# A router in four column groups, exponentials and scores moved one place forward, and the first expert's opening taken out of the expert programs (gated cross-attention with a mixture of experts, float32, one core)

## What is computed

```python
x = x + tanh(g_xattn) * xattn(layernorm(x), ctx)          # 16 heads of 32, 128 keys
xf = (layernorm(x) * ln_gamma + ln_beta).reshape(T, 512)  # T = 4096
logits = clip(xf @ router_w.T, -10000, 10000)             # (T, 8)
top_v, top_i = top_k(logits, 2)
top_p = exp(top_v - max) / sum
# every token goes to 2 of 8 experts, at most 1280 tokens each
gu = einsum('ecd,efd->ecf', xb, w12); h = silu(g) * u
yb = einsum('ecf,edf->ecd', h, w3)
out[tokens] += weights * yb
x = x + tanh(g_ffn) * out
```

## Time and profile before

| | |
|---|---|
| median of 3 runs | 2671.38 us (2670.05 to 2671.79) |
| the profiled execution's own time | 2672.94 us |
| its span, first to last instruction | 2671.2 us |
| PE busy | 2599.4 us, 97% |
| DVE busy | 1362.1 us, 51% |
| ACT busy | 952.6 us, 36% |
| POOL busy | 422.7 us, 16% |
| chain that ended last | PE 88%, DVE 4%, issue 3%, ACT 2%, POOL 1% |
| mean granted PE clock | 0.987 |

### The profile page before, as it was taken

How to read it: one execution, slowest core, us unless ns; L and a number is a source line. 1 busy time by engine, 2 the same in 40 slices (tenths; PEclk the granted TensorE clock), 3 DMA queues, 4 the chain that set the end, 5 groups by cost and what they waited for, 6 DMA issues and landing times.

```text
span 2671.2 us, 40600 instructions
## 1 busy us (share of the span) xinstructions
PE 2599.4 (97%) x14168; PEld 2313.1 (87%) x14169; DVE 1362.1 (51%) x2628; ACT 952.6 (36%) x2498; POOL 422.7 (16%) x399
## 2 busy tenths in 40 slices
PE   7999999699999999999999999999999999999998
PEld 6888887699998888889888788888888999989987
DVE  5888887444444444454444444444434444445555
ACT  6777776222223222232222322322223322233343
POOL 5556565200001000010000200100001100030030
PEclk9999999799999999999999999999999999999999
DMA  8422323321114011140110511221013211142142
GB/s 332 176 97 91 107 80 112 121 88 47 47 36 110 28 43 47 34 116 24 47 47 27 124 48 71 68 71 48 24 47 71 77 47 47 47 90 102 71 128 82
DMA packets 58994, 208.37 MB, mean 78 GB/s; under 512 B 8517, under 2 KB 8797, under 8 KB 50563
## 3 DMA queue, kind: packets, MB, share of 16 engines
q1 hardware_dynamic: 42242, 175.30, 18.2%
q0 software_dynamic: 16640, 31.69, 6.2%
HBM read 145.60 MB, written 67.70 MB: 80 GB/s over the span
## 4 chain that ended last, share of the span: by engine, by line
PE 88%; DVE 4%; issue 3%; ACT 2%; POOL 1%; DMA 1%; another core or an unknown queue 1%; DVEq 0%; SPq 0%; ACTq 0%; POOLq 0%
PE bank L1601 78%; PE bank L947 6%; ACT staged L493 1%; PE bank L1047 1%; PE bank L1607 1%; PE bank L1011 1%; PE bank L1022 1%; DVE before L828 1%; PE bank L1038 0%; DVE neg_max L703 0%; POOL expert_rows L422 0%; POOL staged L389 0%; DVE xT_lo L640 0%; DVE yacc L1541 0%
## 5 line engine op out<-in xcount | busy, mean ns | idle before, releaser
L1561 DVE TENSOR_TENSOR h<-silu,bank 128x384 f32<-128x384 f32 (+2 forms) x320 | 183.8, 574 | 828.0 <-PE bank L1601 818.3
L1601 PE MATMUL bank<-slotsT_hi,early_hi 128*128 128x384 f32 (+2 forms) x1280 | 445.9, 348 | 13.1 <-issue 11.6
L1601 PE MATMUL bank<-slotsT_hi,w_hi 128*128 128x384 f32 (+2 forms) x1280 | 442.3, 346 | 3.2 <-DVE w_lo L1502 3.2
L1601 PE MATMUL bank<-slotsT_hi,early_lo 128*128 128x384 f32 (+2 forms) x1280 | 443.0, 346 | 1.7 <-issue 1.7
L1601 PE MATMUL bank<-slotsT_lo,early_hi 128*128 128x384 f32 (+2 forms) x1280 | 443.5, 346 | 0.0
L1601 PE MATMUL bank<-slotsT_lo,w_hi 128*128 128x384 f32 (+2 forms) x1280 | 442.1, 345 | 0.0
L1601 PE MATMUL bank<-slotsT_hi,w_lo 128*128 128x384 f32 (+2 forms) x1280 | 440.9, 344 | 0.0
L1469 ACT CAST h_hi<-h 128x384 fp32r<-128x384 f32 (+2 forms) x320 | 169.2, 529 | 744.0 <-DVE h L1561 741.1
L1463 ACT ACTIVATE silu<-bank 128x384 f32<-128x384 f32 (+2 forms) x320 | 162.0, 506 | 725.6 <-PE bank L1601 725.0
L1411 POOL DMA_INDIRECT out_dram<-yout,token x63 | 97.9, 1554 | 1969.4 <-ACT yout L1455 1957.9
L1541 DVE TENSOR_TENSOR yacc<-bank,yacc 128x512 f32<-128x512 f32 x464 | 316.6, 688 | 168.8 <-PE bank L1601 167.9
(11 more groups left out here) (199 smaller groups left out, 3508.9 us busy)
## 6 DMA issues: line engine op xcount, KB each, us to landing
staged<-in_moe_w_dram SPq DMA_DIRECT2D x33, 1536.0 KB
raw<-in_moe_w_dram SPq DMA_DIRECT2D x32, 1536.0 KB
xrow<-expert_rows SPq DMA_DIRECT2D x42, 520.0 KB, 8.8
expert_rows<-zeros SPq DMA_DIRECT2D x40, 520.0 KB, 7.8
xin<-in_x_dram SPq DMA_DIRECT2D x17, 512.0 KB, 3.8
xres<-in_x_dram SPq DMA_DIRECT2D x15, 512.0 KB, 3.7
out_dram<-xres SPq DMA_DIRECT2D x15, 512.0 KB
staged<-in_L_xattn_Wq_dram SPq DMA_DIRECT2D x1, 1024.0 KB, 7.2
```

The lines of the kernel that those rows point to most:

```text
L1561: nc.vector.tensor_tensor(h32[q % 2][:, 0:W], silu[q % 2][:, 0:W], UB[q % 2][:, 0:W], ALU.mult)\
L1601: last = nc.tensor.matmul(out_ap, st, mv, start=(at == 0), stop=(at == n - 1))
```

## The change

Four parts. **Router:** `rwT` becomes 32 columns wide (8 of them the router's weights, the rest zero), and `router` is four matmuls, one for each quarter of the features, each with 32 columns of `rwT` as weights and the 256 tokens of `xnT` moving, each into its own 32 partitions of PSUM (columns 256 to 511 of the router's bank). ACT copies the four parts to `parts` (`copy_parts`, 128 x 256), and `logits_made`, two matmuls with `parts` as weights and the 0/1 matrix `pick_expert` moving, adds them up. `pick_expert` is made once at the start by a reduction of `ident` on DVE, and POOL clears `rwT` once. **ACT:** `exps(n, 4)` stands ahead of `a_halves(n-1, 1)`, and `copy_parts` behind that. **DVE:** `maxima(n, 6)` stands ahead of `route(n-2)`. **Experts:** the test at each program's start is gone. `top` tests the index once; for the first expert it leads through a chain of its own to one of eight copies of `opening`, each of which then branches to its program; for all others it leads behind those copies, to a second chain (`later`). In the last blocks the calls are reordered to match, and ACT's rounding of the first expert weights comes after all router work.

```diff
-                    def router(blk, tiles=(0, 1)):
-                        pe.wait_ge(xnT_ready, 2 * blk + tiles[-1] + 1)
-                        for a in tiles:
-                            for k in range(KD):
-                                last = nc.tensor.matmul(l_bank(blk)[:, a * E:(a + 1) * E], xnT[:, a, k, :], rwT[:, k, :],
-                                                        start=(k == 0), stop=(k == KD - 1))
+                    def router(blk):
+                        pe.wait_ge(xnT_ready, 2 * blk + 2)
+                        for k in range(KD):
+                            last = nc.tensor.matmul(parts_bank(blk)[DK * k:DK * (k + 1), :], rwT[:, k, :], xnT[:, :, k, :],
+                                                    start=True, stop=True)
+                        last.then_inc(parts_ready, 1)
+                    def logits_made(blk):
+                        pe.wait_ge(parts_copied, blk + 1)
+                        for a in range(2):
+                            last = nc.tensor.matmul(l_bank(blk)[:, a * E:(a + 1) * E], parts[:, a * P:(a + 1) * P],
+                                                    pick_expert[:, :], start=True, stop=True)
+                        last.then_inc(l_ready, 1)
...
+                    def copy_parts(blk):
+                        act.wait_ge(parts_ready, blk + 1)
+                        if not isinstance(blk, int) or blk > 0:
+                            act.wait_ge(l_ready, blk)
+                        nc.scalar.copy(parts[:, :], parts_bank(blk)).then_inc(parts_copied, 1)
...
                     def whole(nt):
-                        with eng.If(e < 1):
-                            opening()
                         chunk(nt, e, 0, 0, 0, True, False)
...
+                    def opened(nt):
+                        here = eng.mark_branch_hint_location()
+                        opening()
+                        late = f"{name}_{nt}_late"
+                        eng.br_lt(index, E, on_true=f"{name}_{nt}", on_false=late).branch_hint(here)
...
+                    opens, later = f"{name}_opens", f"{name}_later"
+                    eng.br_lt(index, 1, on_true=opens, on_false=later)
+                    with nc.body(opens, valid_engines=mine):
+                        pick(TILES, True)
+                    for nt in TILES[:-1]:
+                        with nc.body(f"{name}_{nt}_opening", valid_engines=mine):
+                            opened(nt)
+                    with nc.body(later, valid_engines=mine):
+                        pick(TILES, False)
+                    for nt in reversed(TILES):
                         with nc.body(f"{name}_{nt}", valid_engines=mine):
                             whole(nt)
```

More of the change, by code:

```diff
@@ L129, in flamingo_gated_layer @@
             gbo_b = sb("gbo_b", [P, D])
-            rwT = sb("rwT", [P, KD, E])
+            rwT = sb("rwT", [P, KD, DK])
+            parts = sb("parts", [P, TB])
+            pick_expert = sb("pick_expert", [P, E])
             wq_hi, wq_lo = (sb(f"wq_{h}", [P, KD, D], f32r) for h in ("hi", "lo"))
@@ L229, in flamingo_gated_layer @@
             l_bank = lambda blk: bank[4] if is_last(blk) else L_BANK
+            parts_bank = lambda blk: l_bank(blk)[:, TB:2 * TB]
             res_of = lambda blk: xin if is_last(blk) else xres
@@ L342, in _ @@
                     nc.gpsimd.memset(neg_half[:, :], -0.5)
+                    nc.gpsimd.memset(rwT[:, :, :], 0.0)
                     nc.gpsimd.memset(before[:, 0, :], 0.0).then_inc(cleared, 1)
@@ L581, in step @@
                             rows_T(n - 2)
+                        if has(n, 0):
+                            exps(n, 4)
                         if has(n, -1):
                             a_halves(n - 1, 1)
+                        if has(n, -2):
+                            copy_parts(n - 2)
                         if has(n, 0):
-                            exps(n, 4)
                             exps(n, 5)
@@ L601, in _ @@
                     rows_T(LAST - 1)
+                    copy_parts(LAST - 1)
+                    rows_T(LAST, (0,))
+                    second_exp(LAST - 1)
+                    rows_T(LAST, (1,))
+                    copy_parts(LAST)
+                    second_exp(LAST)
                     act.wait_ge(raw_loaded[0], 16)
@@ L889, in step @@
                             a_rest(n - 1, 1)
+                        if has(n, 0):
+                            maxima(n, 6)
                         if has(n, -2):
                             route(n - 2)
-                        if has(n, 0):
-                            maxima(n, 6)
                         if has(n, 1):
@@ L1130, in step @@
                             scores(n, 6, b_s)
+                        if has(n, -2):
+                            logits_made(n - 2)
                         if has(n, -1):
@@ L1161, in _ @@
                     turn_rows(LAST, (0,))
-                    router(LAST, (0,))
+                    logits_made(LAST - 1)
                     turn_rows(LAST, (1,))
                     positions(LAST - 1)
-                    router(LAST, (1,))
+                    router(LAST)
+                    logits_made(LAST)
                     positions(LAST)
@@ L1321, in whole, with pick @@
                             nc.br(end, engines=mine)
-                    def pick(sizes):
+                    def opened(nt):
[3 more added lines that the diff above has]
+                        eng.br_lt(index, E, on_true=f"{name}_{nt}", on_false=late).branch_hint(here)
+                        with nc.body(late, valid_engines=mine):
+                            nc.br(f"{name}_{nt}", engines=mine)
+                    def pick(sizes, first):
                         if len(sizes) == 1:
-                            whole(sizes[0])
+                            if first:
+                                opened(sizes[0])
+                            else:
+                                nc.br(f"{name}_{sizes[0]}", engines=mine)
                             return
-                        more = f"{name}_over_{sizes[0]}"
-                        eng.br_lt(n_e, sizes[0] * P + 1, on_true=f"{name}_{sizes[0]}", on_false=more)
+                        more = f"{name}_{first}_over_{sizes[0]}"
+                        chosen = f"{name}_{sizes[0]}_opening" if first else f"{name}_{sizes[0]}"
+                        eng.br_lt(n_e, sizes[0] * P + 1, on_true=chosen, on_false=more)
                         with nc.body(more, valid_engines=mine):
-                            pick(sizes[1:])
-                    pick(TILES)
-                    for nt in reversed(TILES[:-1]):
+                            pick(sizes[1:], first)
+                    opens, later = f"{name}_opens", f"{name}_later"
[8 more added lines that the diff above has]
+                    for nt in reversed(TILES):
                         with nc.body(f"{name}_{nt}", valid_engines=mine):
```

12 lines of the change are left out of this document (4 added, 8 removed).

## The result

| | before | after |
|---|---|---|
| median | 2671.28 us (4 runs) | 2702.09 us (4 runs, 2697.41 to 2704.47) |
| ratio | | 1.0114, 95% interval 1.0096 to 1.0131 |
| span of the profiled execution | 2671.2 us | 2700.4 us |
| mean granted PE clock | 0.987 | 0.980 |
| starts of the positions of the third block and of the fourteenth (L1056, now L1079) | 150.39, 447.83 | 148.12, 435.34 |

The change makes the kernel slower by 31 us, where 2.2 were forecast (2673.6, range 2656 to 2683). (The head's time is that of PE's load of the expert's count.) Up to the head of expert 0 the change gains 8.8 us; expert 0 gives 4.0 back; the seven others take 34.0 more: 29.2 together, the difference of the spans.

What follows compares the result with a forecast made beforehand. PE, busy for 97% of the span, was taken to bound the kernel. Stage one -9.1, tail +0.3 and experts +11.0 summed to +2.2 us, forecasting a median of 2673.6 us, range 2656 to 2683.

Steps and rivals of the forecast that it cites:

- The first test: Head of experts 1 to 7: jump to the second chain's page costs a 3.40 us fetch; pauses 1.7 at 1, 2, 4.
- What goes with the first test: Stage two: expert pauses 5.1 + 0.8 + 3.5 + 0.6 plus clock 1, summing to +11.0 us.
- The wait for `w_lo` at expert 7: PE's 3.21 us wait for DVE would vanish, DVE being done by then; expert 7 nets +0.6 us.
- The clock: PE in stage two: at most experts 1, 2 and 4 get a new slow stretch; +1 us, ends 0 and +5.
- Expert 0: Between the first opening and its program a branch stays, now with a hint; costed at nothing.
- Stage one: Router saves 0.87 us a step less 0.20 more stalls, over 14 steps -9.1 us; with the tail's +0.3.
- late queries: Stage one on PE: stalls of 0.46 us a step from late words would grow to 0.66.
- the tail: Last block's uncovered router: copy 0.5 and sums 0.4 against 1.3 saved, first weights rounded later; +0.3 us, between -1 and +1.
- The two moves: Stage one: `exps(n, 4)` moved ahead on ACT and `maxima(n, 6)` on DVE, both costing nothing.
- The resident page: Rival, chance 0.25: second chain's page stays at hand or is read ahead; experts about -5 us, total 2657.6 us.
- the chain that binds: Rival, chance 0.10: POOL's `add_bias`, `norm`, DVE's places and scatter make the step; stage one gains 0, total 2682.7 us.
- the stalls vanish: Rival, chance 0.10: later scatter falls where nobody waits for PE's word; stage one -18.6 us, total 2664.1 us.

Runs made afterwards that it cites:

- the padded runs: Never-run PE instructions added ahead of the expert loop: 166 or 133 to one opening, 67 to the kernel before; 2663.13, 2694.24 and 2679.89 us.
- one opening: The change with the eight opening copies replaced by a single tested opening in the head, ahead of the chain of before; 2663.05 us, ratio 0.9969.
- the router alone: The change's stage one with the function `experts` of the kernel before; 2662.19 us, ratio 0.9964.
- a second trace of before: The kernel before, unchanged, executed and profiled again; 2673.96 us, usual step 26.65 us.
- the runs with 166 and with 133 dead instructions: One opening with 166 or 133 never-run PE instructions ahead of the expert loop; 2663.13 us (ratio 0.9970) and 2694.24 us (ratio 1.0084).
- openings last: The change with the second chain right behind the head's test, then the programs, and the first expert's chain and openings at the end; 2671.09 us, ratio 1.0001.
- experts alone: The kernel before with the change's function `experts`, stage one as before; 2702.63 us, ratio 1.0121.

## Why the prediction was wrong

- **The first test.** Right, and to the number: 3.38 us against 3.40, at all seven experts; pauses of 1.60 and 1.76 at experts 1 and 2 against 1.7; the packets as forecast (between 1143 and 1483 us nine, none before). That PE holds eight pages is now shown by the padded runs, which the prediction could only count out; the nine packets during expert 2 say that the change needs nine.
- **What goes with the first test** is the step that failed: +11.0 us for the experts, measured +34.0 from expert 1 on and 4.0 more at expert 0. The pauses were to grow by 10.0 (5.1 + 0.8 + 3.5 + 0.6) and grew by 24.7, the clock was to cost 1 and cost 9.3. I held that "Only the head's page is announced by a hint" and let the return be free. At the ends of experts 3 and 6 it wasn't, 2.98 and 5.31 us, and with the first test behind it nothing was left to hide either. Expert 4 paused 4.18 for 1.7 forecast, expert 7 12.12 for about 6.5. The pause of 2.73 us inside expert 1 came over ACT, which the prediction left out. ACT has a head of its own, and its load of the count starts 3.3 us behind its return's branch, where before it was 0.3: a fetch, by all that the trace shows. Its first work for expert 1 comes after 6.04 us of "issue", where before it was 1.12, its slots are late, then DVE's, then PE's. The wait for `w_lo` at expert 7, which I struck out with 3.2 us, stayed at 3.26: DVE is led by PE's products and was as late as PE.
  ACT's row for that, timeline of ACT after and then before, head of expert 1:

```profile
812.81 1.28 ACT L1507 ACT_TABLE_LOAD   x1 [6.04 <-issue]
```

```profile
812.75 1.28 ACT L1463 ACT_TABLE_LOAD   x1 [1.12 <-issue]
```

- **The clock** was the other mis-sized term: +1 forecast. Against 1.00 behind the pause of 1.74 in the earlier trace rows stand 0.50 behind 1.76, 1.98 and 4.18 in the change. The pauses explain 41.3 - 16.6 = 24.7 of the 34.0; the remaining 9.3 is what the extra stretches at the lower clock come to: in the profiled executions PE worked some 33 us of stage two from expert 1 on at 0.50 in place of 14, and half of the difference of 19 is 9.7. The length of a pause alone doesn't tell whether the clock falls: in one opening 2.75 us at expert 6 left it at 1.00 (2369 to 2371 us).
- **Expert 0** was put at nothing. Its opening now ends in a jump to the program, which took 6.67 us of the sequencer although a hint stood 10 us ahead of it, and a pause of 5.85 for one of 1.5 before. The fetch of before, 3.69 us on the chain, lay ahead of the opening and hid behind its wait for data.
- **Stage one.** The sum was -9.1 + 0.3 = -8.8, and the head of expert 0 came 8.8 us sooner, the router alone 8.2 to 9.2 by its medians: right in size, but by luck, for two errors cancel in it. The step, forecast at 26.4 to 26.6, came at 26.1. I took 0.46 us of late queries a step as a property of the kernel and let them grow to 0.66. They are gone in a second trace of before, and in the change. By that trace the gain a step is 0.54: 1.26 for the router, less 0.36 for the sums, 0.29 for the turned rows that wait for DVE, and small ones both ways. By the trace that I read it is 1.06. That `route` would start about 3.0 us behind the router was right (2.99); that PE's words would come later still for it was not. And the tail, +0.3 forecast, took back more: against the first trace of before 12.5 us ahead at the positions of 435.34, 8.6 at the last ones (against the second 9.4 and 6.1). Timeline of PE there, after:

```profile
459.49 0.66 PE L1055 MATMUL bank<-ident,row 128*128 128x128 f32 x4 [2.11 <-DVE row L809]
...
463.63 0.60 PE L1079 MATMUL bank<-chosen,upper 128*128 128x16 f32 x2 [1.62 <-DVE before L834]
...
466.17 1.02 PE L1071 MATMUL bank<-pick_expert,parts 128*128 128x8 f32 x4 [0.49 <-ACT parts L531]
470.00 0.61 PE L1079 MATMUL bank<-chosen,upper 128*128 128x16 f32 x2 [2.81 <-DVE before L834]
```

  With nothing else to do, PE waits for DVE and ACT at each link of the router's now longer way.
- **The two moves** were costed at nothing, the copy of the parts too. That was right only for router and moves together: the moves without the new router cost 0.7 us a step, the new router without the moves 1.15.
- **The rivals.** The resident page is out (seven stalls), so is the chain that binds (26.1 a step). That the stalls vanish came true of the step, but not by the change, since they are missing in a second trace of before too, and its 18.6 us for stage one didn't come. None of the four had the case that came, in which returns miss as well and the clock falls near every head.

The window of two pages that the Trainium skill gives (page "Runtime: NRT & Kernel Launch", section "Instruction fetch mechanics") doesn't hold for PE here: eight stay. Its 128 KiB for PE in blocks of 16 KiB do hold: between the runs with 166 and with 133 dead instructions lies the step from eight pages to nine, and eight packets of 16.4 KB are that size.

What stays open: why the returns missed are those behind programs of seven and five tiles in the change, of nine tiles in openings last and of ten tiles in the padded runs with nine pages, though each has its hint; and why the hint ahead of the first opening didn't save the fetch at expert 0.

## What to carry to other kernels

Count pages, not instructions: if a loop's head and its longest body together just fit the engine's instruction memory, one more page between them makes every pass fetch everything, and the price is each jump's fetch, some of the returns' too, and the clock behind many of the pauses. Code that runs once belongs beside or behind what the loop runs, and not between its head and its body. And look at a second trace of the kernel before a small repeated stall is made a term of the sum; test reordered calls and the work that they are to cover as a pair and apart, for neither may gain alone.

## What was not expected of the hardware

- 33 dead instructions more or fewer, ahead of a loop that never runs them, move this kernel by 31 us (2663.13 and 2694.24).
- A fetch behind a jump took PE's sequencer 3.0 to 3.7 us for the jump over the eight openings (13 of them, in the change and in experts alone), 3.0 to 5.3 us for a missed return, and up to 6.7 and 6.8 for the jump from an opening to its program; a branch hint before it did not always help.
- Two executions of the same program differ by 0.5 us in the usual step of stage one (27.18 and 26.65) and by 1 us in all (2672.94 and 2673.96).
- A pause of 1.74 us left the granted clock at 1.00 in one trace; pauses of 1.76 and 1.98 were followed by stretches at 0.50 in another, and one of 2.75 left it at 1.00 in a third (2663.32 us, one opening).
